# A parted PSUM ring and value products in one run, in an attention stage between two mixtures of experts

## What is computed

```python
x = L0_attn_x                                   # 4 x 1024 tokens x 128, float32
x = x + 0.5 * ffn(layernorm(x))                 # mixture of 8 experts, top 2
x = x + attn(layernorm(x))
x = x + 0.5 * ffn(layernorm(x))

def attn(x, W_qkv, W_o):                        # 16 heads of 8
    qkv = (x @ W_qkv.T).reshape(b, n, 16, 8).transpose(0, 2, 1, 3)
    score = softmax(einsum('bhif,bhjf->bhij', qkv, qkv) / sqrt(8), axis=-1)
    attn = einsum('bhij,bhjf->bihf', score, qkv)
    return attn.reshape(b, n, 128) @ W_o.T
```

## Time and profile before

| | us |
|---|---|
| median of 3 runs | 1316.57 (1316.5 to 1319.73) |
| the profiled execution | 1308.1, span 1306.4 |
| busy PE, DVE, ACT, POOL in the span | 1150.1, 1126.8, 887.6, 482.2 |
| first score product, last score product | 363.6, 1058.2 |

### The profile page before, as it was taken

How to read it: one execution, slowest core, us unless ns; L and a number is a source line. 1 busy time by engine, 2 the same in 40 slices (tenths; PEclk the granted TensorE clock), 3 DMA queues, 4 the chain that set the end, 5 groups by cost and what they waited for, 6 DMA issues and landing times.

```text
span 1306.4 us, 27214 instructions
## 1 busy us (share of the span) xinstructions
PE 1150.1 (88%) x9031; PEld 630.4 (48%) x9031; DVE 1126.8 (86%) x2337; ACT 887.6 (68%) x1879; POOL 482.2 (37%) x545
## 2 busy tenths in 40 slices
PE   3847999888589999999999999999998889999993
PEld 2746888777123223223323223233322258788882
DVE  7877888877899999989998999999999368988885
ACT  1223555555168999898888888898887965455651
POOL 3873547334113000324235313333333117543232
PEclk9999999999679999999999999999999999999997
DMA  8124665564010200002001010001000503554654
GB/s 277 50 70 171 215 212 187 206 215 134 29 50 19 67 6 15 18 18 63 5 27 37 11 32 19 18 26 28 18 5 24 181 31 138 191 204 181 247 199 139
DMA packets 58617, 123.55 MB, mean 95 GB/s; under 512 B 12352, under 2 KB 33826, under 8 KB 58448
## 3 DMA queue, kind: packets, MB, share of 16 engines
q1 hardware_dynamic: 49488, 103.83, 23.1%
q0 software_dynamic: 8704, 16.93, 4.1%
q10 hardware_dynamic: 288, 1.05, 0.2%
HBM read 36.66 MB, written 23.88 MB: 46 GB/s over the span
## 4 chain that ended last, share of the span: by engine, by line
PE 56%; DVE 25%; issue 5%; POOL 5%; ACT 5%; DMA 3%; SPq 1%; DVEq 0%; POOLq 0%; ACTq 0%
PE psum L2286 14%; DVE att_neg_part L1970 12%; PE psum L2264 8%; PE psum L2200 8%; PE psum L2188 7%; PE psum L2190 7%; PE psum L2247 5%; POOL rows_dram L1263 4%; DVE att_neg_part L1975 2%; DMA ffn_block_rows<-rows_dram 2%; DVE ffn_x2c L1911 2%; DVE stats L1604 2%; ACT att_probs L1456 2%; DVE ffn_hidden L1922 1%; PE psum L2309 1%
## 5 line engine op out<-in xcount | busy, mean ns | idle before, releaser
L1456 ACT ACTIVATE att_probs<-psum 128x512 f32<-128x512 f32 x1024 | 554.9, 599 | 59.3 <-PE psum L2268 31.2
L1970 DVE TENSOR_REDUCE att_neg_part<-psum 128x2 f32<-128x1024 f32 x443 | 519.1, 1216 | 33.3 <-PE psum L2248 31.6
L2286 PE MATMUL psum<-att_probs,att_values 128*16 128x256 f32 x4096 | 322.1, 386 | 12.4 <-ACT att_o_t L1471 7.7
L1424 ACT ACTIVATE ffn_silu<-ffn_x2c,ffn_rec 128x256 f32<-128x256 f32 (+1 forms) x320 | 154.6, 487 | 170.1 <-DVE ffn_x2c L1911 170.0
L1279 POOL DMA_INDIRECT y_dram<-ffn_y,ffn_block_rows x144 | 142.4, 989 | 235.0 <-ACT ffn_y L1442 206.5
L2268 PE MATMUL psum<-att_right,att_left 64*128 64x512 f16 x512 | 199.5, 390 | 17.3 <-DVE att_neg_part L1970 13.2
L2247 PE MATMUL psum<-att_right,att_left 62*128 62x512 f16 x512 | 198.4, 388 | 15.6 <-DVE att_neg_part L1970 10.1
L2264 PE MATMUL psum<-att_right,att_left 64*128 64x512 f16 x512 | 199.5, 390 | 8.5 <-DVE att_neg_part L1970 6.8
L2248 PE MATMUL psum<-att_right,att_left 62*128 62x512 f16 x512 | 200.0, 391 | 0.0
L1911 DVE TENSOR_SCALAR ffn_x2c<-psum,ffn_rec 128x256 f32<-128x256 f32 (+1 forms) x320 | 162.8, 513 | 36.7 <-PE psum L2190 33.0
L2188 PE MATMUL psum<-ffn_block_t,ffn_rec 128*128 128x256 f32 (+1 forms) x640 | 179.0, 362 | 1.2 <-ACT ffn_block_t L1375 1.2
(11 more groups left out here) (238 smaller groups left out, 1176.6 us busy)
## 6 DMA issues: line engine op xcount, KB each, us to landing
ffn_rec<-record SPq DMA_DIRECT2D x80, 776.5 KB, 3.9
ffn_block_rows<-rows_dram SPq DMA_DIRECT2D x64, 130.0 KB, 3.1
record<-in_L_ffn_W SPq DMA_DIRECT2D x16, 256.0 KB, 6.5
att_left<-q_parts_dram SPq DMA_DIRECT2D x64, 64.0 KB, 2.2
y_dram<-ffn_y,ffn_block_rows POOLq DMA_INDIRECT x144
x_sb<-in_L_attn_x SPq DMA_DIRECT2D x4, 512.0 KB, 7.0
record<-in_L_ffn_Wo SPq DMA_DIRECT2D x8, 256.0 KB, 7.2
rows_dram<-rows,place_i POOLq DMA_INDIRECT x128, 2.4
```

Source lines behind the costliest of these rows:

```text
L1456: S.activation(probs[:, slot % PROBS, :], ring_bank(("score", slot))[:, :], ACT.Exp, scale=unlift).then_inc(att_bank.by_act, 1)
L1970: last = V.tensor_reduce(out=neg_part[:, h % 2, keys, p::PAIR, t], in_=psum[:, low:high + 1, :], axis=AX.X, op=ALU.max, negate=True)
L2286: last = TE.matmul(value_bank[head * VS:head * VS + VW, q], values[:, b % 2, kt, team * TEAM + head, :], probs[:, (UNIT * n + j) % PROBS, ...
```

## The change

The ring of seven is parted in two rings. Banks 0 to 3 (`max_bank`) are for the maximum units alone, two units at a time, always in neighbouring banks. Banks 4 to 6 (`att_bank`) are for scores and for the chores that held a bank of the ring. The reduction in two pieces (L1975) falls away, since two banks are always adjacent. A maximum unit now waits only for the reduction of the unit two before. A score or chore waits for the holder three places before it in its own ring, always one that ScalarE gives back.

The value products of a unit are no longer issued in two parts behind the next unit's two pairs: both parts follow, in one run, the second pair (and its maximum unit). The chores stand where they stood. Nothing that is computed changes.

```diff
--- before.py
+++ after.py
@@ -57,8 +57,8 @@
 
 
 
-    def __init__(self, banks, filled, by_act, maxed, reduced):
-        self.banks = banks
+    def __init__(self, first, banks, filled, by_act, maxed, reduced):
+        self.first, self.banks = first, banks
         self.filled, self.by_act, self.maxed, self.reduced = filled, by_act, maxed, reduced
         self.at, self.number, self.holders = {}, {}, []
         self.count = {1: 0, 2: 0}
@@ -71,7 +71,7 @@
         self.number[name] = (size, self.count[size])
 
     def bank(self, name, k=0):
-        return (self.at[name] + k) % self.banks
+        return self.first + (self.at[name] + k) % self.banks
 
     def full(self, name):
         size, n = self.number[name]
@@ -449,7 +449,9 @@
 
         route_bank = [Banks([bank[b]], semaphore(f"route_full{b}"), semaphore(f"route_emptied{b}"))
                       for b in range(B)]
-        att_bank = Ring(7, semaphore("bank_full"), semaphore("bank_emptied"), maxed, reduced)
+        MAX_BANKS = 2 * PAIR
+        max_bank = Ring(0, MAX_BANKS, None, None, maxed, reduced)
+        att_bank = Ring(MAX_BANKS, 7 - MAX_BANKS, semaphore("bank_full"), semaphore("bank_emptied"), None, None)
 
 
         side_bank = Banks([value_bank], semaphore("side_full"), semaphore("side_emptied"))
@@ -590,7 +592,7 @@
 
         def max_banks(n):
 
-            return [att_bank.bank(("max", n), k) for k in range(PAIR)]
+            return [max_bank.bank(("max", n), k) for k in range(PAIR)]
 
         PLACINGS = 2 * NTEAM
 
@@ -762,7 +764,7 @@
 
 
         for n in range(MAX_FIRST):
-            att_bank.plan(("max", n), 2)
+            max_bank.plan(("max", n), 2)
             if n == HALF_UNITS + 1:
                 for chore in first_chores:
                     plan_banks(*chore)
@@ -1966,15 +1968,8 @@
             h = 2 * i + g
             V.wait_ge(maxed, n + 1)
             low, high = max_banks(n)
-            if high == low + 1:
-                last = V.tensor_reduce(out=neg_part[:, h % 2, keys, p::PAIR, t], in_=psum[:, low:high + 1, :],
-                                       axis=AX.X, op=ALU.max, negate=True)
-            else:
-
-                for k, where in enumerate((low, high)):
-                    last = V.tensor_reduce(out=neg_part[:, h % 2, keys, PAIR * k + p, t:t + 1], in_=bank[where],
-                                           axis=AX.X, op=ALU.max, negate=True)
-            last.then_inc(reduced, 1)
+            V.tensor_reduce(out=neg_part[:, h % 2, keys, p::PAIR, t], in_=psum[:, low:high + 1, :],
+                            axis=AX.X, op=ALU.max, negate=True).then_inc(reduced, 1)
             if n % HALF_UNITS == HALF_UNITS - 1:
                 V.wait_ge(reduced, n + 1)
                 if h >= 2:
@@ -2224,8 +2219,9 @@
                 tensor_scores(slot)
                 for n in max_units(slot + 1):
                     tensor_row_max(n)
-                if slot >= UNIT:
-                    tensor_values(slot // UNIT - 1, slot % UNIT // 2)
+                if slot >= UNIT and slot % UNIT == UNIT - 2:
+                    for part in range(2):
+                        tensor_values(slot // UNIT - 1, part)
                 for chore in chores[slot] + chores[slot + 1]:
                     tensor_chore(*chore)
             for part in range(2):
@@ -2239,7 +2235,7 @@
                     TE.wait_ge(max_rows_set, i + 1)
                 TE.wait_ge(lefts_in[s], lefts_before(i))
                 TE.wait_ge(rights_in[s], rights_before(i))
-            for emptied in att_bank.empty_before(("max", n)):
+            for emptied in max_bank.empty_before(("max", n)):
                 TE.wait_ge(*emptied)
             low, high = max_banks(n)
             q = slice((g * HT + t) * P, (g * HT + t + 1) * P)
```

## The result

| | before | changed |
|---|---|---|
| median, us | 1318.15 (4 runs) | 1369.49 (4 runs, 1365.78 to 1371.51) |
| ratio | | 1.0387, 95% interval 1.0361 to 1.0412 |
| the profiled execution, us | 1308.1 | 1365.78, span 1364.0 |
| first to last score product, us | 694.6 | 743.4 |

A forecast was written before the change was run, and what follows sets the result against it. A loop of waits through TensorE and ScalarE was taken to bound scoring: 11.3 + 616.8 + 28.1 + 61 + 14 + 8 gave 739 us for 694.6, so 1316.6 + 45 = 1362 us, range 1332 to 1399.

The forecast's parts named there:

- The loop: Units without chores: first score, its exponential, fourth score, second maximum product, value run, next first score in series: 2.57 us.
- The units without maxima: The last 13 units of scoring, which have no maximum units: 2.34 us each, counted 12 times as 28.1 us.
- The first three units: Start of scoring, while the clock still rises from half speed: they keep their 11.3 us.
- The chores: Extra work in scoring: 61 us for products on TensorE, 14 for ScalarE's copies, 8 for clumps of VectorE's other work.
- e0: First of a unit's four exponentials on ScalarE: starts 0.43 us after the first score, lasts 0.60; value_bank's copy delays it about 0.1.
- s0: First of a unit's four scores on TensorE; the next unit's follows the value run, 1.00 us after the run starts.
- The sum: All terms of scoring: 739 us in place of 694.6, or +45, added to the median shown of 1316.6.
- A: Rival: the third score bank does not bind, VectorE limits, units without chores stay at 2.24 to 2.34: 1299 us, chance 0.07.
- B: Rival: units with chores absorb the surplus almost whole, hardly any change: 1317 us, chance 0.02.
- C: Rival: with three banks chores cost more, up to one exponential for each of 110 holders: 1421 us, half 1392; chance 0.08.
- E: Rival: TensorE's idle time halves its clock in a fifth of the units, 77 us more: 1439 us, chance 0.04.
- s3: Fourth of a unit's scores, in the second pair on TensorE: waits for the first exponential's end, about 1.03 after the first score.

The follow-up runs named there:

- with the run first: The parted rings with the value run moved behind the next unit's first pair, against the changed kernel's second: 1380.4 us, ratio 1.0475 to the kernel before.
- `three_max_banks`: The changed kernel with three banks for maxima and four for scores and chores: 1601.4 us, ratio 1.2251 to the kernel before.
- the fourth bank: Changed kernel cut to one maximum product a unit, with four score and chore banks instead of three: 1291.9 us against 1327.1 with three.
- `maxima_first`: The changed kernel with the maximum unit issued ahead of the two scores in each unit's second pair: 1342.3 us, ratio 1.0171 to the kernel before.

## Why the prediction was right

**The loop** (its first part): the unit without chores was put at 2.57 and is 2.60. Four links are right to 0.01 (0.43, 0.60, 0.22 or 0.23, 0.31), the run is 0.99 and was put at 1.00. One link was mis-sized: from the end of the exponential to the waiting product 0.00 was taken, from the earlier trace rows, and it is 0.055 to a score product, in 246 of 256 units of the changed kernel, and 0.15 to the maximum product of the ring of seven. Over 240 units this is 13 us, against which stand 2 or 3 us of the run and as much of the second maximum product; 7 are left. The one row was no measurement of that link, though the profile names the copy L1483 as what ended the wait. Counted by the order of holders, the maximum unit at 518.89 stands behind the second score of 516.51 and the maximum unit of 516.74, and not behind the bank that was copied; and that unit's reduction ended at 518.75, 0.14 before, which is the price of such a release in this ring:

```profile
517.53 1.22 DVE L1970 TENSOR_REDUCE att_neg_part<-psum 128x2 f32<-128x1024 f32 x1
```

**The units without maxima** were put at 2.34 and are 2.38, for the same link. Two starts, and the wait between:

```profile
1084.50 0.39 PE L2260 MATMUL psum<-att_right,att_left 64*128 64x512 f16 x1
...
1085.57 0.39 PE L2264 MATMUL psum<-att_right,att_left 64*128 64x512 f16 x1 [0.47 <-ACT att_probs L1458]
...
1086.88 0.39 PE L2260 MATMUL psum<-att_right,att_left 64*128 64x512 f16 x1
```

**The first three units** kept 11.3 us in the sum and took 9.0: the first of the three took 2.26 us where it took 3.41. It is 2.26 in the parted rings with two parts and with the run first too, and 3.40 to 3.41 in the rings of seven, so the parting is what did it. **The chores** were summed at 61 + 14 + 8 = 83 us. Measured: 743.4 less 9.0, 240 x 2.60 and 12 x 2.38 leaves 82. That is a remainder and doesn't show each part by itself. The parts of one finish:

```profile
484.34 0.59 ACT L1473 COPY att_o_t<-psum 128x512 f32<-128x512 f32 x1 [0.24 <-PE psum L2282]
...
484.82 2.07 ACT L1458 ACTIVATE att_probs<-psum 128x512 f32<-128x512 f32 x4
...
487.00 0.66 PE L2305 MATMUL psum<-identity,att_o_t 128*128 128x128 f32 x4
...
487.69 0.59 ACT L1478 COPY att_o_t<-psum 128x512 f32<-128x512 f32 x1 [0.80 <-PE psum L2305]
...
488.18 1.09 ACT L1458 ACTIVATE att_probs<-psum 128x512 f32<-128x512 f32 x2
```

From the transpositions to the next exponential 1.18 (487.00 to 488.18) where 1.16 was worked out; the copy of `value_bank` at 484.34 puts e0 at 484.82, where s0 at 484.21 would have let it start at 484.63: 0.2 late and not 0.1.

**The sum** for scoring was 739 and is 743.4. By scoring alone the loss is 48.8 us. The two profiled executions lie 57.7 apart; the other 9 us stand outside scoring, in stages that the change doesn't touch: the first score is at 367.9 instead of 363.6, and from the last score to the end 252.7 us pass instead of 248.2. The runs point to the chip more than to the change. From the first maximum product to the first score product 28 to 29 us pass in both, so the 4.3 us lie ahead of attention. And the time ahead of the first maximum product together with the time after the last score is 583 to 585 us in the four kernels profiled on the chip where the kernel before takes 1306.9, and 588 to 598 in the six profiled on the chips where it takes 1317.6 and 1318.6, whatever their rings and runs; the one on the other chip of 1306.8, `three_max_banks`, has 588, which this doesn't explain. The kernel before was profiled at 1308.1 with 583.6, the changed one with 591.8. On which chips these two profiles were taken is not known, and why chips differ stays open; but the sum's base of 1308.1 and its 8.5 us to the median fit a difference between chips. The medians, 51 apart, lie within 3 us of scoring's 48.8. So the forecast was 4 us short in scoring: 7 by the pace of a unit, less 2 by the first three units and 1 by the chores.

**The rivals.** A (the third bank doesn't bind) falls by the wait of L2264 and by the fourth bank's 35 us. B falls by the interval. C would have shown in the units with chores, which cost what was summed. D likewise. E falls: the granted clock was 1.00 in every stretch of 10 us from 380 to 1110, at a lower load of TensorE. What the Trainium skill (TensorE: Matmul & The Clock Gate, A second HAM failure mode: psum-queue depth-cycling) tells of another kernel, a clock that goes back and forth, did not happen here. The Trainium skill (TensorEngine Tiling (Array Packing), Key Properties) says that a change of tiling mode drains TensorE, and the rows agree, 0.31 against 0.22. The run does save such passages, with 0.99 for both parts against 2 x 0.55. The trace shows why that is no gain: TensorE waits in the same unit for longer than it saves.

**Of what would show it**, the list came true: s3 at 1.08 after s0 (1.03 forecast), ScalarE's gap before e0 (0.53 us, about 0.4 forecast), L1970's successor idle 80.3, 75.8 of it behind L2244 (over 70 forecast), a run of 16 with 0.99 to the next score, and no L1975. The last score was at 1111 and not 1103.

## What to carry to other kernels

Taken from the runs here: count buffers against the longest stretch of the queue that goes without a new result, not against the mean. If a producer issues n results between two long runs and has fewer than n buffers, then one buffer's whole round (product, reader, release) and the run stand in series, wherever in the order the run is put, while every engine shows idle time. Write such a loop down link by link from starts in the timeline, look at it from each buffer's holder and not from one, and compare it with the busiest engine's own time before batching: saving switches on the engine that waits brings nothing, while the same run gained 0.30 us a unit where nothing waited.

## What the runs showed of the hardware

A wait's release has a price, and it doesn't go by the engine that releases. From the end of a ScalarE reader to a waiting score product it is 0.055 us. From the end of a VectorE reduction to a waiting maximum product it is 0.057 in `maxima_first` (165 times; 507.97 + 1.16 to 509.19 above) and in the changed kernel, but 0.146 in `three_max_banks`. From the end of a ScalarE reader to a waiting maximum product it is 0.145 in the ring of seven with the run. What the two dear cases have in common is that the unit's two banks had two different holders, so that two waits stand ahead of the product where the others have one; the number of waits alone was not varied. And a product that seemed free, since it ran beside another in the other half of the array's rows, was not: where its partner came late, leaving it out took 0.21 us out of the chain (0.53 to 0.32 from s3 to the run), because the two pairs stood staggered, one product after the other.
